# An attention-and-MLP block on one core: the state's product in 32x32 tiles, the last part of the out product and the residual addition moved

## What is computed

```
xn = layernorm(x)
Q = xpos(xn @ W_Q);  K = xpos(xn @ W_K, downscale);  V = xn @ W_V         # per head
scores = (Q @ K.T) * D          # D[n, m] = gamma_h ** (n - m) for n >= m, else 0
Y = groupnorm_per_head(scores @ V) * gn_weight + gn_bias
attn = (silu(xn @ W_G) * Y) @ W_O
q = fp4_quant_dequant           # per 16 elements
h = silu(q(xn) @ q(w_gate).T) * (q(xn) @ q(w_up).T)
out = x + attn + q(h) @ q(w_down).T
```

## Time and profile before

| | |
|---|---|
| median of 3 runs | 902.4 us (901.42 to 902.75) |
| profiled execution, its own time | 902.86 us |
| its span | 901.1 us |
| granted PE clock, mean | 0.991 of full speed |
| busy: PE, DVE, POOL, ACT | 868.1 (96%), 834.8 (93%), 679.6 (75%), 495.2 us (55%) |

### The profile page before, as it was taken

How to read it: one execution, slowest core, us unless ns; L and a number is a source line. 1 busy time by engine, 2 the same in 40 slices (tenths; PEclk the granted TensorE clock), 3 DMA queues, 4 the chain that set the end, 5 groups by cost and what they waited for, 6 DMA issues and landing times.

```text
span 901.1 us, 20383 instructions
## 1 busy us (share of the span) xinstructions
PE 868.1 (96%) x7698; PEld 763.9 (85%) x7698; DVE 834.8 (93%) x1883; ACT 495.2 (55%) x1370; POOL 679.6 (75%) x795
## 2 busy tenths in 40 slices
PE   2889999999999999999999999999999999999996
PEld 1768888888888888888888888888888888888885
DVE  7879999999999999999999999999999999999984
ACT  5655555555555555555555555555555555555542
POOL 4767787777778777777877877787787777778774
PEclk9899999999999999999999999999999999999999
DMA  9200110110111011011101101100110110110000
GB/s 339 73 1 19 36 37 19 36 37 22 32 36 36 19 37 36 20 35 36 33 23 36 36 19 37 36 31 25 36 37 19 36 37 24 31 37 12 8 13 18
DMA packets 30049, 33.62 MB, mean 37 GB/s; under 512 B 3328, under 2 KB 28672, under 8 KB 29696
## 3 DMA queue, kind: packets, MB, share of 16 engines
q1 hardware_dynamic: 29808, 32.26, 11.4%
q10 hardware_dynamic: 144, 0.07, 0.0%
HBM read 23.92 MB, written 8.39 MB: 36 GB/s over the span
## 4 chain that ended last, share of the span: by engine, by line
PE 93%; POOL 3%; DVE 2%; ACT 1%; issue 1%; DMA 0%; POOLq 0%; DVEq 0%
PE quad L899 12%; PE quad L901 12%; PE quad L900 12%; PE quad L1080 5%; PE quad L961 4%; PE quad L984 4%; PE bank L901 3%; PE bank L900 3%; PE bank L899 3%; PE bank L1017 3%; PE quad L1087 3%; PE quad L926 3%; PE quad L1064 3%; PE quad L985 2%; PE quad L949 2%; PE quad L953 2%
## 5 line engine op out<-in xcount | busy, mean ns | idle before, releaser
L899 PE MATMUL quad<-w_gu_hi,xqT_hi 128*128 128x512 f32 (+1 forms) x384 | 150.3, 391 | 0.9 <-DVE xqT_lo L592 0.9
L901 PE MATMUL quad<-w_gu_hi,xqT_lo 128*128 128x512 f32 (+1 forms) x384 | 144.4, 376 | 0.0
L900 PE MATMUL quad<-w_gu_lo,xqT_hi 128*128 128x512 f32 (+1 forms) x384 | 143.3, 373 | 0.0
L463 POOL TENSOR_TENSOR rstd<-var_eps,power 128x9 f32<-128x9 f32 x67 | 124.1, 1853 | 5.6
L452 POOL TENSOR_TENSOR x_quot<-xn,x_inv 128x256 f32<-128x256 f32 x64 | 40.4, 632 | 90.9 <-DVE x_inv L640 90.9
L471 POOL TENSOR_TENSOR xT_lo<-xT_in,xT_hi 128x256 fp32r<-128x256 f32 x64 | 47.4, 740 | 61.7 <-ACT xT_hi L789 61.7
L438 POOL TENSOR_TENSOR h_quot<-h,h_inv 128x704 f32<-128x704 f32 x64 | 88.8, 1388 | 6.3 <-DVE h_inv L583 1.3
L721 ACT ACTIVATE xqT_hi<-bank 128x256 fp32r<-128x256 f32 x64 | 24.6, 384 | 121.1 <-PE bank L934 121.1
L448 POOL TENSOR_TENSOR qk<-qk_cos,qk_sin 128x512 f32<-128x512 f32 x64 | 82.8, 1293 | 7.6 <-PE bank L971 0.9
L487 POOL TENSOR_TENSOR gate_gn<-gate,gn 128x512 f32<-128x512 f32 x64 | 83.3, 1301 | 0.2 <-ACT gate L782 0.2
L901 PEld LDWEIGHTS quad<-w_gu_hi,xqT_lo 128*128 128x128 f32 x384 | 72.5, 189 | 11.5
(11 more groups left out here) (178 smaller groups left out, 2953.6 us busy)
## 6 DMA issues: line engine op xcount, KB each, us to landing
x_in<-in_x_dram SPq DMA_DIRECT2D x64, 128.0 KB, 2.1
xT_in<-in_xT_dram SPq DMA_DIRECT2D x64, 128.0 KB, 2.2
out_dram<-y_out SPq DMA_DIRECT2D x64, 128.0 KB, 1.7
sin<-const_sin_dram SPq DMA_DIRECT2D x1, 1792.0 KB, 10.9
raw<-in_w_gu_dram SPq DMA_DIRECT2D x2, 512.0 KB, 6.5
w_qkvg<-in_w_qkvg_dram SPq DMA_DIRECT2D x1, 1024.0 KB, 7.3
cos<-const_cos_dram SPq DMA_DIRECT2D x1, 896.0 KB, 7.0
raw<-in_w_down_dram SPq DMA_DIRECT2D x2, 352.0 KB, 7.7
```

Of the source, the lines that this page charges most:

```text
L463: pool.tensor_tensor(rstd[:, (t + 3) % RING, 0:1 + H], var_eps[:], power[:], ALU.pow).then_inc(rstd_ready, 1)
L899: pe.matmul(out, hi[:, k], w_hi[:, k], start=start, stop=False)
L900: pe.matmul(out, hi[:, k], w_lo[:, k], start=False, stop=False)
L901: return pe.matmul(out, lo[:, k], w_hi[:, k], start=False, stop=stop)
```

## The change

The compact state is used as it is. `state_sum` becomes `state`, the block-diagonal matrix, its clearing on POOL and the four copies on ACT for each kept tile (with their semaphore `state_copy`) go. The product is eight matmuls of 32x32 tiles in place of two of 128x128. So that the eight stand on eight different tiles of the array, the heads of the second group lie one quarter of the partitions further in q, k, their tables and the state (`ORDER`, `place`); this costs nothing at run time, since the weights are permuted on the host. The product moves from in front of x's transposes to directly in front of y's product, and its waits for `state_copy` and `masked1` go, as its place behind the wait for `masked0` covers them.

The last two matmuls of the out product move from the end of a step to the next step, behind the Q and K product and in front of the transposes of x and z. The addition of x on DVE moves behind the masking of the first two heads of each group and `h_inv`.

```diff
+ORDER = [*range(HG), *(HG + (r - 1) % HG for r in range(HG))]
...
-        for h in range(H):
+        for h in ORDER:
...
+        def quarter(r):
+            return slice(r * HD, (r + 1) * HD)
+
+        def place(g, r):
+
+            return quarter((r + g) % HG)
...
-                if exists(i - 1) and kept(i - 1):
-                    t = i - 1
-                    if t == 0:
-                        act.wait_ge(cleared, 3)
-                    act.wait_ge(kv_add, kept_upto(t))
-                    for r in range(HG):
-                        rows = slice(r * HD, (r + 1) * HD)
-                        ins = act.activation(tiles(state[:])[rows, :, rows], heads(state_sum[:])[rows], ACT.Copy)
-                    ins.then_inc(state_copy, 1)
...
-                if exists(i - 1) and later(i - 1):
-                    t = i - 1
-                    pe.wait_ge(state_copy, kept_upto(t - 1))
-                    pe.wait_ge(masked1, t + 1)
-                    for g in range(G):
-                        ins = pe.matmul(b_yT[g], state[:, g * P:(g + 1) * P], qT[:, g, :], start=True, stop=False)
-                    ins.then_inc(st_ready, 1)
+                if exists(i - 3):
+                    t = i - 3
+                    for k in range(KD):
+                        ins = pe.matmul(b_out, zT_lo[:, k], w_out_hi[:, k], start=False, stop=k == KD - 1)
+                    ins.then_inc(out_ready, 1)
...
+                if exists(i - 1) and later(i - 1):
+                    t = i - 1
+                    for g in range(G):
+                        for r in range(HG):
+
+                            rows = place(g, r)
+                            ins = pe.matmul(b_yT[g][quarter(r), :], state[rows, g * HD:(g + 1) * HD], qT[rows, g, :], start=True, stop=False)
+                    ins.then_inc(st_ready, 1)
...
-                if exists(i - 2):
-                    t = i - 2
-                    for k in range(KD):
-                        ins = pe.matmul(b_out, zT_lo[:, k], w_out_hi[:, k], start=False, stop=k == KD - 1)
-                    ins.then_inc(out_ready, 1)
```

More of the change, by code:

```diff
@@ L140, in block_kernel @@
         probs = sb("probs", [P, HG, G * P])
-        state_sum = sb("state_sum", [P, G * HD])
-        state = sb("state", [P, D])
+        state = sb("state", [P, G * HD])
         yT = sb("yT", [P, D])
@@ L223, in block_kernel @@
         x_peak = sem("x_peak")
-        summed = sem("summed")
         masked0 = sem("masked0")
         h_inverted = sem("h_inverted")
+        summed = sem("summed")
         rope_sin = sem("rope_sin")
@@ L283, in block_kernel @@
         x_high = sem("x_high")
-        state_copy = sem("state_copy")
         x_normed = sem("x_normed")
         qk_ready = sem("qk_ready")
-        st_ready = sem("st_ready")
+        out_ready = sem("out_ready")
         x_turned = sem("x_turned")
@@ L293, in block_kernel @@
         h1_turned = sem("h1_turned")
+        st_ready = sem("st_ready")
         yT_ready = sem("yT_ready")
@@ L307, in block_kernel @@
         s_ready = sem("s_ready")
-        out_ready = sem("out_ready")
         def exists(t):
@@ L424, in _ @@
             pool.memset(moments[:], 1.0).then_inc(cleared, 1)
-            pool.memset(state[:], 0.0).then_inc(cleared, 1)
-            pool.wait_ge(cleared, 3)
+            pool.wait_ge(cleared, 2)
             def step(i):
@@ L570, in step @@
                     dve.tensor_reduce(x_max[:], blocks(xn[:, t % 2, :]), AX_X, ALU.max, apply_absolute_value=True).then_inc(x_peak, 1)
[L571 to L576, removed]
                 if exists(i - 1):
@@ L583, in step @@
                     dve.tensor_scalar(h_inv[:], h_rec[:], SIX, 1e12, ALU.mult, ALU.min).then_inc(h_inverted, 1)
+                if exists(i - 3):
+                    t = i - 3
+                    dve.wait_ge(out_ready, t + 1)
+                    if t >= 2:
+                        dve.wait_ge(stored, 16 * (t - 1))
+                    dve.tensor_tensor(y_out[:, t % 2, :], b_out, x_in[:, t % SLOTS, :], ALU.add).then_inc(summed, 1)
                 if exists(i):
@@ L617, in step @@
                     if t == 0:
-                        dve.wait_ge(cleared, 3)
+                        dve.wait_ge(cleared, 2)
                     dve.wait_ge(x_stats, t + 1)
@@ L667, in step @@
                     if t % CHUNKS == 0:
-                        dve.tensor_copy(state_sum[:], b_kv[:, 0:G * HD]).then_inc(kv_add, 1)
+                        dve.tensor_copy(state[:], b_kv[:, 0:G * HD]).then_inc(kv_add, 1)
                     else:
-                        dve.tensor_tensor(state_sum[:], state_sum[:], b_kv[:, 0:G * HD], ALU.add).then_inc(kv_add, 1)
+                        dve.tensor_tensor(state[:], state[:], b_kv[:, 0:G * HD], ALU.add).then_inc(kv_add, 1)
                 if exists(i):
@@ L876, in load_functions @@
             def load_functions():
-                act.wait_ge(cleared, 3)
+                act.wait_ge(cleared, 2)
                 act.activation(scratch[:], power[:], ACT.Silu)
@@ L959, in step @@
                         for r in range(HG):
-                            rows, head = slice(r * HD, (r + 1) * HD), (g * HG + r) * HD
-                            ins = pe.matmul(b_yT[g][rows, :], val[:, head:head + HD], probs[:, r, g * P:(g + 1) * P],
+                            head = (g * HG + r) * HD
+                            ins = pe.matmul(b_yT[g][quarter(r), :], val[:, head:head + HD], probs[:, (r + g) % HG, g * P:(g + 1) * P],
                                             start=t % CHUNKS == 0, stop=True)
@@ L969, in step @@
                         for r in range(HG):
-                            rows, head = slice(r * HD, (r + 1) * HD), (g * HG + r) * HD
-                            ins = pe.matmul(b_kv[rows, g * HD:(g + 1) * HD], qk[:, D + head:D + head + HD], val[:, head:head + HD],
+                            key, head = D + g * P + place(g, r).start, (g * HG + r) * HD
+                            ins = pe.matmul(b_kv[place(g, r), g * HD:(g + 1) * HD], qk[:, key:key + HD], val[:, head:head + HD],
                                             start=True, stop=True)
@@ L1193, in layouts @@
     heads = lambda w: w.transpose(0, 2, 1).reshape(D, D)
+    w_q, w_k = w_q[ORDER], w_k[ORDER]
     w_gu = [w[c * GW:min((c + 1) * GW, F)] for c in (2, 1, 0) for w in (w_gate, w_up)]
```

## The result

The changed kernel takes 905.05 us in the median (904.13 to 906.23, 8 runs), the kernel before 901.92 us in the runs beside it (901.34 to 903.11, 8 runs). The ratio is 1.0031, with a 95% interval of 1.0022 to 1.0040: about 3 us slower. 905.0 was predicted. The runs of one kernel spread with the clock that PE was granted: of the kernel before, twelve runs at a mean of 0.998 took 901.2 to 901.8 us and four at 0.989 took 904.1 to 905.2, so a difference of 1 us between two medians can come from the clock alone.

What follows compares the result with a forecast made beforehand. PE was taken to bound the kernel (13.23 us a step). -0.30 + 0.35 = +0.05 us over 56 steps, +2.8, less 0.3 at the end, gave 905.4; the median, 0.46 lower, 905.0 us; range 896 to 915.

Steps and rivals of the forecast that it cites:

- The front: State product gone from before x's and z's transposes on PE: 0.33 us saved, 0.11 lost waiting for z; -0.30 a step taken.
- rival 4: z's transposes on PE: z comes in time after all, without the 0.11 us wait; 897.1 us, chance 7%.
- X: Time on PE from the new state product's start to y's product's start; 0.35 us taken: two rounds and a pause.
- rival 2: New state product runs in rounds of four: three rounds and a pause 911.7 us, four 916.7 us; chance 25%.
- rival 1: No pause between the tiled state product and y's product, X = 0.25 us; 899.3 us, chance 25%.
- Rival 3: State product's tiles of one group don't run together, since the four write one PSUM bank; 990 us, chance 3%.
- The out product and the addition: Last two out matmuls behind the Q and K product, x's addition later on DVE: cost 0 a step.
- The end: Step 64, where PE waits for DVE's mask: the mask starts 0.33 us earlier, -0.3 us once.

Runs made afterwards that it cites:

- the same-tiles experiment: Changed kernel without the rotation, the second group's four 32x32 products on the same four tiles as the first group's; 914.71 us, ratio 1.0133 to the kernel before.
- the column tiles: Changed kernel's order, but the state product as eight matmuls on 128x32 column tiles from the block-diagonal state, ACT copies back; 908.54 us, ratio 1.0063 to the kernel before.
- The moves alone: Kernel before with only the last two out matmuls behind the Q and K product and x's addition behind h_inv; 903.46 us, ratio 1.0017.
- an early z: Changed kernel with z's addition in front of gate_gn, state product as two whole-array matmuls in front of y's product, ACT copies back; 902.59 us, ratio 1.0005.
- the tiles at the old place: Kernel before with only the state product changed to eight 32x32 tiles, between the Q and K product and x's transposes; 907.45 us, ratio 1.0060.
- z earlier: Changed kernel with z's addition on POOL moved in front of gate_gn; 897.53 us, ratio 0.9945 to the kernel before.

## Why the prediction was right, point by point

- **The front, -0.30 us.** In the mean of the regular steps it is 4.017 us before from the scores to y's product, and 4.055 - 0.377 = 3.678 after without X: 0.34 less; the rest of the step is 0.016 longer. Together -0.32. The 0.30 was read from one early step of 12.93; such steps have 12.91 in the mean, which would have given -0.33. The wait for z is shown: taking it away gave 0.12 us a step, 7.5 us, which is rival 4's condition brought about by an edit. That the time met rival 4's (897.1 estimated, 897.5 measured) is partly luck: the step fell 0.06 us under the kernel before and not 0.09, since X is longer and the front shorter than in its sum.
- **X.** 0.35 was taken, 0.377 measured: rounds of 0.13 and 0.11, 0.03 of issue, a pause of 0.11. Two rounds of eight: shown by the starts of the records and by the same-tiles experiment; rival 2 (rounds of four, 911.7 to 916.7 us) describes that experiment and not the change. The pause into y's product: shown by the column tiles, which have none; rival 1 falls with it.
- **Rival 3**, the tiles of a group one after another, didn't happen. The four tiles of a group lie in four row groups and write one PSUM bank, and run at once. The rule of the Trainium skill, TensorEngine Tiling, section Gotcha 1: PSUM Pressure, doesn't hold in that form here, where each row tile writes partitions of its own in the bank. What row tiles in one bank and the same partitions do was not tried.
- **The out product and the addition, 0.** The moves alone made the step 0.02 us longer, and it stands behind K.T @ V: from there to the next scores 8.773 us, 8.756 in the kernel before, 8.772 in the changed kernel. It doesn't belong to the moves alone: with them and an early z it is 8.762, without them, in the tiles at the old place, 8.783. In all of them it arises a few thousandths at a time in the first down, gate and up products. I did not find what it is; in the steps without a state product of the kernel before it is there too (8.769), so it was in the 0.30.
- **The end, -0.3.** In the changed kernel the scores of step 64 start at 882.75 and the last transposes of z at 894.51, 11.76 us; in the kernel before it is 12.04 us. So -0.28:

```profile
880.97 0.73 PE L1080 MATMUL quad<-qT,kT 32*128 32x128 f32 x16
...
893.01 0.69 PE L944 MATMUL bank<-ident,z 128*128 128x128 f32 x2 [4.75 <-POOL z L432]
```

The profiled execution did not keep it. Behind these transposes, for which PE had waited 4.75 us (4.65 in the changed kernel), PE runs at 1.2 GHz and then at 2.4, and it stayed at the lower clock longer in the changed kernel. The 6.00 us behind their start, of the kernel before and of the changed kernel (31 matmuls each, granted clock 0.74 and 0.64):

```profile
893.00:899.00 6.00, 5.47 (x31) 4.92 (x31) 1.94 (x5) 1.37 (x3) 0.00 (x0) 0.74 0.06 22
```

```profile
894.50:900.50 6.00, 5.95 (x31) 5.41 (x31) 1.52 (x5) 1.36 (x3) 0.00 (x0) 0.64 0.06 22
```

The last out matmuls start 5.07 us behind the transposes before and 5.55 after, 0.48 later, so from the scores of step 64 to the end it is 20.1 us before and 20.3 after. Whether other executions kept the 0.28 is not shown.

- **The sum.** 56 x 0.055 = 3.1, less 0.3, is +2.8 us; measured +3.1 (901.92 to 905.05). The mechanism held, and its main parts (the wait for z, the rounds, the pause) have an experiment each; that 905.0 was met so closely is luck. X was 0.03 higher than taken (+1.5 us) and the front 0.02 better (-1.3 us), and these errors nearly cancel; the median of the kernel before is 0.5 lower with more runs than the 902.4 from which 905.0 was reckoned; and the clock can move a median by as much.

## What to carry to other kernels

Before a piece is taken off the busiest engine, ask what it covers: here 0.44 us of work hid a z that came 0.05 us late without it, and a quarter of the gain (0.12 us) went into that wait. One POOL operation moved past another whose result nobody stood waiting for gave it back, and made of a change that lost 0.3% one that gains 0.5%. Small tiles pay for each change of shape: put them beside other tiled products, on tiles that differ, and count the pauses before the rounds.

## What the runs showed of the hardware

- A change between tile shapes on PE costs 0.09 to 0.11 us, also between 32x32 and 128x32 tiles, and none is seen between two products in 128x32 tiles; back from 32x32 tiles to the whole array the next two transposes took 0.28 us in place of 0.22.
- Eight fp32 matmuls on eight different 32x32 tiles run together: their sixteen records start within 0.18 us in two rounds, though the four of a group write one PSUM bank. On four tiles it takes four rounds of 0.115.
- A transpose whose operand comes 0.05 us late costs 0.10 to 0.12 us in all: 0.05 of waiting, and 0.27 in place of 0.22 until the next transposes. The weight load of z's transposes starts 0.11 us ahead of their matmul where z is in time (418.81 and 418.92 with z earlier) and right at it in the changed kernel (both at 408.98 to 408.99), so it isn't hidden.
- PE's clock: near the start, behind a wait of 1.6 us, PE ran on at 1.2 GHz for about 3 us in the profiled execution of the kernel before, and at 2.4 GHz in that of the changed kernel. From the scores of the first tile to those of the second it took 17.8 us there and 16.2 in the other nine profiled executions, so a single profile can be 1.6 us off for the clock alone. The same holds for the end, where it was 0.5 us.
